# Values of layer zero: all high parts of a block first, then the low parts, each pair behind its own wait

## The reference, cut to what matters

```
h = h + L0_attn(layernorm(h))          # group norm, then:
q, k, v = x @ wq + bq, x @ wk + bk, x @ wv + bv
scores  = einsum("bqhd,bkhd->bhqk", q, k) * 64 ** -0.5
attn    = softmax(scores)
out     = einsum("bhqk,bkhd->bqhd", attn, v) @ wo + bo + residual
h = h + L0_ffn(layernorm(h))
h = h + L1_attn(layernorm(h))          # 8 heads of width 16
h = h + L1_ffn(layernorm(h))           # 16 experts, a capacity for each
```

## Time and profile before

| | |
|---|---|
| time, median of 3 runs | 6748.31 us (6740.82 to 6760.65) |
| the profiled execution's own time | 6749.96 us |
| its span, first to last instruction | 6748.1 us |
| PE busy | 6073.5 us (90%) |
| PE weight loads busy | 4046.7 us (60%) |
| DVE busy | 4525.4 us (67%) |
| ACT busy | 3214.0 us (48%) |
| POOL busy | 2465.6 us (37%) |
| mean granted TensorE clock | 0.948 |

### The profile page before, as it was taken

One profiled execution on the slowest core, in us unless ns is written; L12 is line 12 of the kernel. 1 busy time (PEld: TensorE's weight loads), 2 busy tenths in 40 slices (PEclk: granted clock), 3 DMA queues, 4 the chain that ended last, 5 costly groups with the idle time before them and its releaser, 6 DMA issues.

```text
span 6748.1 us, 127182 instructions
## 1 busy us (share of the span) xinstructions
PE 6073.5 (90%) x40167; PEld 4046.7 (60%) x40167; DVE 4525.4 (67%) x11162; ACT 3214.0 (48%) x6321; POOL 2465.6 (37%) x2215
## 2 busy tenths in 40 slices
PE   6789898998989989898998989989898998989986
PEld 4656665656656666665656656666665656656643
DVE  4466676676767767676776767767676776767664
ACT  2345555445444444544545445444544445454541
POOL 2534333433333333333433333333333433333300
PEclk7899999999999999999999999999999999999987
DMA  2121211212222121211212222121211212221110
GB/s 60 41 68 42 59 42 38 64 39 53 49 55 48 40 50 45 59 42 38 64 40 52 49 55 49 40 50 45 59 42 38 64 33 59 49 54 42 25 30 9
DMA packets 98048, 317.03 MB, mean 47 GB/s; under 512 B 27782, under 2 KB 32854, under 8 KB 87126
## 3 DMA queue, kind: packets, MB, share of 16 engines
q1 hardware_dynamic: 97366, 308.41, 19.7%
HBM read 57.19 MB, written 41.94 MB: 15 GB/s over the span
## 4 chain that ended last, share of the span: by engine, by line
issue 47%; POOL 27%; PE 17%; DVE 6%; DMA 1%; POOLq 1%; ACT 1%; SPq 1%; DVEq 0%; ACTq 0%
POOL pr_lo L508 22%; PE bank L883 3%; POOL on L1264 3%; PE bank L911 2%; PE bank L869 2%; PE bank L946 2%; DVE mxh L1640 2%; PE bank L930 1%; DMA stacks<-parts 1%; PE bank L931 1%; DVE z L1428 1%; POOL rs L1235 1%; PE bank L793 1%; PE bank L909 1%; PE bank L956 1%
## 5 line engine op out<-in xcount | busy, mean ns | idle before, releaser
L1640 DVE TENSOR_REDUCE mxh<-bank 128x1 f32<-128x512 f32 x4096 | 2789.9, 687 | 1710.2 <-PE bank L883 1682.2
L1141 ACT ACTIVATE pr<-bank 128x512 f32<-128x512 f32 x4096 | 2419.4, 598 | 2713.8 <-PE bank L911 2669.6
L883 PE MATMUL bank<-stacks 128*128 128x512 f32 x4096 | 2225.5, 544 | 335.2 <-DVE mxh L1640 231.8
L508 POOL TENSOR_TENSOR pr_lo<-pr 128x1024 bf16<-128x1024 f32 x960 | 1824.3, 1901 | 1168.9 <-ACT pr L1141 1168.6
L911 PE MATMUL bank<-stacks 65*128 65x512 f32 (+1 forms) x4096 | 1667.7, 407 | 5.0 <-ACT pr L1141 5.0
L883 PEld LDWEIGHTS bank<-stacks 128*128 128x128 f32 x4096 | 801.3, 196 | 1122.2 <-DVE mxh L1640 804.7
L930 PE MATMUL bank<-v,pr 128*128 128x129 bf16 x8192 | 1079.9, 224 | 54.1 <-POOL pr_lo L508 53.5
L931 PE MATMUL bank<-v,pr_lo 128*128 128x129 bf16 x8192 | 1067.7, 222 | 0.0
L930 PEld LDWEIGHTS bank<-v,pr 128*128 128x128 bf16 x8192 | 787.9, 99 | 348.4 <-issue 306.3
L1264 POOL TENSOR_TENSOR on<-on,o_r 128x128 f32<-128x128 f32 x512 | 235.3, 460 | 2015.7 <-DVE on L1670 2015.6
L911 PEld LDWEIGHTS bank<-stacks 65*128 65x128 f32 (+1 forms) x4096 | 801.6, 196 | 225.0 <-issue 61.7
(11 more groups left out here) (171 smaller groups left out, 5070.9 us busy)
## 6 DMA issues: line engine op xcount, KB each, us to landing
stacks<-parts SPq DMA_DIRECT2D x384, 512.0 KB, 6.5
stacks<-parts_d SPq DMA_DIRECT2D x224, 128.0 KB, 3.0
parts_d<-mx SPq DMA_DIRECT2D x16, 1024.0 KB, 4.5
stacks<-parts_d SPq DMA_DIRECT2D x224, 64.0 KB, 2.8
stage<-in_pe SPq DMA_DIRECT2D x16, 512.0 KB, 8.0
stacks<-mrow SPq DMA_DIRECT2D x512, 2.0 KB
parts_d<-on SPq DMA_DIRECT2D x16, 512.0 KB, 5.3
parts_d<-stage SPq DMA_DIRECT2D x16, 512.0 KB, 6.2
```

The source lines that it names most:

```text
L508: return eng.tensor_tensor(low_of(u, kt - 1).rearrange("p a b -> p (a b)"), w, hi, ALU.subtract)
L883: mm(maxb[k % 2][:, :], qs[:, t * P:(t + 1) * P], ks[:, g * HALF:(g + 1) * HALF], start=True, stop=True).then_inc(max_filled.sem, 1)
L1141: act.activation(pr[:, at % 2, kt, :], score[k % 2][:, :], ACT.Exp, scale=SCALES[layer]).then_inc(exp_done.sem, 1)
L1640: dve.tensor_reduce(mxh[:, layer, n // 2, n % 2:n % 2 + 1], maxb[k % 2][:, :], AX_X, ALU.max)\
```

## The change

Inside a block the order of the 16 matmuls changes, for all four blocks of a unit: first the 8 with high parts, then the 8 with low parts. In block `j = 0` the wait for all low parts goes. A wait for the unit's eight probability tiles stands in front of the block, and each pair of low parts has a wait of its own in front of its first matmul: the first for one POOL instruction of the unit, the second for two, and so on; for units 0 to 3 the fourth pair waits for DVE's `lo_last` instead. What is added up is the same, in another order. No other engine's program changes.

```diff
@@ values0, block j of the unit before
                 if j == 0 and u % 4 == 0 and u > 0:
                     await_drained(te, seg, f"v0c{u // 4}.0", f"v0c{u // 4}.1")
-                if j == 0:
-                    te.wait_ge(lo_done.sem, lo_done.at(seg.l0, LO_DONE[u + 1]))
-                    if u < LEAD:
-                        te.wait_ge(lo_last.sem, lo_last.at(seg.l0, u + 1))
                 if j % 2 == 0:
                     te.wait_ge(o_drained.sem, o_drained.at(seg, n - 1))
+                if j == 0:
+                    te.wait_ge(exp_done.sem, exp_done.at(seg, 8 * at + T))
                 dst = obank[n % 2][:, (j % 2) * 256:(j % 2) * 256 + w]
                 for kt in range(T):
                     hi = pr[:, at % 2, kt, j * P:(j + 1) * P].bitcast(BF16).rearrange("p (q two) -> p q two", two=2)[:, :, 1]
+                    mm(dst, hi, v0[:, head // 2 % 2, kt, head % 2, 0:w], start=(kt == 0), stop=False)
+                for kt in range(T):
+                    if j == 0 and kt == 6 and u < LEAD:
+                        te.wait_ge(lo_last.sem, lo_last.at(seg.l0, u + 1))
+                    elif j == 0 and kt % 2 == 0:
+                        te.wait_ge(lo_done.sem, lo_done.at(seg.l0, LO_DONE[u] + kt // 2 + 1))
                     lo = low_of(u, kt - kt % 2)[:, kt % 2, j * P:(j + 1) * P]
-                    mm(dst, hi, v0[:, head // 2 % 2, kt, head % 2, 0:w], start=(kt == 0), stop=False)
                     last = mm(dst, lo, v0[:, head // 2 % 2, kt, head % 2, 0:w], start=False, stop=(kt == T - 1))
```

## The result

| | runs | median us | range us |
|---|---|---|---|
| before | 4 | 6751.26 | 6740.82 to 6760.65 |
| after | 4 | 6688.01 | 6685.04 to 6691.63 |

The ratio is 0.9907 (95% interval 0.989 to 0.9924), 63 us less. A second timing on another chip gave 6683.46 us against 6751.02, ratio 0.9898 (0.9882 to 0.9915). The forecast was 6703 us: the direction and the place were right, and the gain came out 17 us larger than the 46 forecast (16 by the means of all executions).

The account below looks back on a forecast made before the run. PE's own work (busy 90%) was taken as the bound. Of 64.2 us stall, 48.7 would go, 95% kept: 46; 6749.96 - 46 = 6704, less 1.65 for the median, 6703 us; 8-in-10 range 6688 to 6744.

Parts of the forecast that it names:

- The place of the wait: Block j = 0: only the last two matmuls stand behind the fourth low part; 14 steps, 0.80 us, run while POOL works.
- How much each stall shrinks: 63 PE stalls at blocks j = 0: each shrinks by the smaller of itself and 0.80 us, together 48.7 of 64.2 us.
- What is kept: Behind the block PE sets the pace and others have slack, so 95% of the gain is kept, 46 us.
- The rest before the fifteenth matmul: Block j = 0: about 0.2 us of each stall remains; L934 shows 10 to 16 us in some 55 waits.
- The price of the added waits: 960 waits added at blocks j = 0: taken as 0, bounds 0 and 0.10 us each, 96 us in all.
- The slower rival: Waiting loads between bf16 matmuls stand exposed, 0.10 us for each of 1024 waits, 102 us; time 6806; chance 0.09.
- Order of the weights: Neighbouring matmuls in a block share the kind of weights: taken as 0, bound 16 us either way over 16384 steps.
- swallowed downstream: Rival: PE waits instead for DVE's maxima, losing between half and all of the 46 us; 6727 to 6750; chance 0.14.
- The turn of loop: Times between starts of turns in loop should fall from 406 to about 403.6 us.
- the likeliest case: The forecast itself, 6703 us for the whole kernel, with its own range 6690 to 6720; chance 0.70.

Follow-up runs that it names:

- e1: Against the kernel before: high parts first, then low parts, the one wait for all low parts still in front; 6748.30 us against 6748.13, ratio 0.9999.
- e2: Against the kernel before: high and low parts still alternate, but each pair waits for its own low part; 6695.45 us, ratio 0.9929.
- e3: Against the kernel before: high parts first, one wait for all low parts before the ninth matmul; 6741.38 us, ratio 0.9996.
- e6: Against the changed kernel: last low pair of block j = 0 moved to the front of block j = 1; 6684.64 us, ratio 0.991 to before.
- e5: Against the changed kernel: the same waits also in blocks j = 1, 2 and 3, 3072 more, always satisfied; 6690.76 us, ratio 0.9915 to before.
- e10: Against the changed kernel: seven overwritten matmuls added ahead of block j = 1 in 61 blocks; 6739.97 us, ratio 0.9988 to before.

## Why the prediction was right, and what it lacked

- **The place of the wait: right, shown.** e1 has the new order and the old wait and gains nothing, e2 has the new waits and the old order and gains 40 us at one clock. The matmuls that can run before the last low part decide it: none (e1), 8 (e3), 12 (e2), 14 (after) gain -1, 25, 40 and 47 us at one clock. e6, which moves the last pair further, gains 56.
- **How much each stall shrinks: right, slightly low.** I had 64.2 us of stall and 48.7 taken from it; by starts it was 67.4 us and 53.6 taken (67.4 - 13.8). Of the 4.9 us that I was low, some 2.7 are PE's faster answer to POOL in `loop`, which I had kept at 0.13 us.
- **What is kept: too high, and the two errors cancel.** At one clock 46.6 us of the 53.6 are kept, 87% and not 95%, with an error of some 2 us. I forecast 46. The missing part is in `loop`. In each of the two traces before and the two after, take off 0.38 us for each us at half clock, an estimate by the fit above: `loop` is then 5122.9 and 5124.3 us long before, 5097.1 and 5096.8 after. That is 26.7 us less, where its stalls by starts shrank by some 33.5; I had 31.1 shrunk and 29.5 kept. What took the other 7 us is not shown.
- **The rest before the fifteenth matmul: right in size, wrong in where it is seen.** By starts 11.3 us stand inside the blocks, in the 10 to 16 forecast, in about as many blocks as the 55 that I had. The wait row of L934 shows 2.5 us in 2 waits, and the forecast said this row would show it. I had noted that the profile's drawn ends hide 0.17 us of a stall, and did not apply it to a rest of 0.2.
- **The price of the added waits: right.** 0 was taken for 960 waits; e5 measured about 1 ns or less each on 3072. The Trainium skill's figure of 50 to 100 ns for reading a semaphore ("Advanced Engine Details and Errata", section "Network/Comms") does not apply to a satisfied wait in front of a weight load here. The slower rival needed 45 ns and is refuted.
- **Order of the weights: right,** 0 (e1: 1 us at one clock).
- **The rival "swallowed downstream" is refuted as forecast.** It had half or more of the gain lost, and at one clock 87% is kept. PE's wait for the maxima is 232.9 us against 231.8, and in the row of the weight loads, which shows short gaps too, it rose by 0.4 to 5 us. A smaller loss of this kind may be part of the 7 us that are missing in `loop`.
- **A term was missing: the granted clock.** The sum held it fixed. Over the executions before had .9488 and after .9519, and 3.1 x 5.04 = 15.6 us is what separates 46.6 us from the 62.4 between the means. I had the row, 0.948 for the profiled execution, and gave it no term and no width. With e10 it is shown that the sign could as well have been the other: a version 25 us slower at one clock would have lost another 27. My own range of 6690 to 6720 for the likeliest case held no such width, and the time fell outside it. It is inside the wider range of 6688 to 6744 by 0.01 us, and by luck: I had placed that lower end for a gain of 14 us by the order, which e1 shows to be nothing.
- **The turn of loop:** forecast 403.6 us, measured (6003.1 - 756.9) / 13 = 403.55. Before it was (6051.6 - 782.1) / 13 = 405.3, not 406, so in this pair of profiles it fell by 1.8 and not by 2.4; in the second pair (406.0 and 403.6) it fell by 2.3, and at one clock by 2.05. In the first pair `loop` had 386 us at half clock before and 393 after; the clock's gain in them came in the stretches around `loop`, 309 us at half clock against 263.

## What to carry to other kernels

Where an engine that runs in order waits for a late input, count the instructions that could stand between the wait and the use; the stall shrinks by their time or by all of it, whichever is smaller, and here 87% of that was kept. A satisfied wait cost 1 ns or less here, so it could be placed wherever it is first needed. Before a difference of under 1% is explained by waits, set the time of every run against its granted clock, compare at one clock, and give the forecast a width for it. A version that is slower than its waits would have it (e3) may have nothing wrong at the place that was changed.

## What the runs showed that was not expected

- 0.001 of the mean granted clock is worth 5 us here, and versions of one kernel that differ only in a few waits or matmuls have means from .9450 to .9528. That is 39 us, nearly as much as the change itself.
- The same instructions, behind 4 us of the same work with the same idle times (0.27 and 0.98 us), ran at 2.4 GHz in one version and at 1.2 in another, with L710's four matmuls at 0.60 and 1.05 us.
- Filling 50 us of PE's idle time with matmuls left the clock where it was (.9488 and .9493).
- In `loop` PE started 0.129 us behind the end of the `pr_lo` that it waited for with the old wait, and 0.058 us with the new ones (medians of 47 and 28 blocks). e1 turned this round, with the wait for all low parts in front again, but written behind the one for `o_drained`: 0.056 us in `loop` and 0.145 in the segments without turns.
